# Ternary weight blocks transposed by DMA instead of TensorE, and another order in the first units of an FFN, in a fused GNN and FFN kernel

## The reference, cut to what matters

```
a = layernorm(x)
neigh = segment_sum(a[src], dst) / max(degree, 1)
h = leaky_relu(a @ W_self + neigh @ W_neigh + b)
x = x + h / max(norm(h), 1e-12)
wq = clip(round(w / scale), -1, 1) * scale      # scale: mean of |w| over 128 columns of a row, + 1e-5
y = layernorm(x)
x = x + (silu(y @ wq_gate.T) * (y @ wq_up.T)) @ wq_down.T
```

## Time and profile before

| | |
|---|---|
| median of 3 runs | 355.49 us (355.23 to 357.14) |
| the profiled execution | 353.95 us |
| its span, first to last instruction | 352.1 us |
| mean granted TensorE clock | 0.989 |
| PE busy | 330.3 us, 94% |
| DVE busy | 302.0 us, 86% |
| ACT busy | 237.6 us, 67% |
| POOL busy | 168.1 us, 48% |

### The profile page before, as it was taken

The page is one execution under the profiler, slowest core; times in us unless marked ns, Lnnn a source line. Parts: engine busy times, 40 slices in busy tenths (PEclk is TensorE's granted clock), DMA queues, the critical chain, the costliest instruction groups (busy, mean ns, idle before and its releaser), DMA issues.

```text
span 352.1 us, 5881 instructions
## 1 busy us (share of the span) xinstructions
PE 330.3 (94%) x1639; PEld 247.7 (70%) x1639; DVE 302.0 (86%) x782; ACT 237.6 (67%) x639; POOL 168.1 (48%) x234
## 2 busy tenths in 40 slices
PE   8999999999989999999569999999999999999991
PEld 3443545544444676877458898989989898899991
DVE  3799998998976269997886999999999989999993
ACT  2287887888992236765567767867668686776660
POOL 6033000000001940110023396889898888899992
PEclk9999999999999999999888999999999999999999
DMA  7982222222231011100000000000000000000205
GB/s 216 295 216 62 65 62 84 60 89 83 71 103 33 3 30 52 53 2 0 1 2 0 1 2 0 3 0 2 1 2 2 0 2 0 2 2 0 92 28 175
DMA packets 9470, 16.69 MB, mean 47 GB/s; under 512 B 1120, under 2 KB 1944, under 8 KB 9436
## 3 DMA queue, kind: packets, MB, share of 16 engines
q1 hardware_dynamic: 9358, 16.21, 15.9%
q10 hardware_dynamic: 78, 0.08, 0.1%
HBM read 13.73 MB, written 2.56 MB: 46 GB/s over the span
## 4 chain that ended last, share of the span: by engine, by line
PE 52%; DVE 13%; ACT 2%; issue 2%; POOL 1%; DVEq 0%; ACTq 0%
PE bank L1381 40%; PE bank L1312 5%; DVE tq_d L961 2%; DVE bn L1116 2%; DVE x_sb L1113 2%; PE bank L1270 1%; DVE z L1095 1%; PE bank L1294 1%; DVE z L1101 1%; PE bank L1359 1%; DVE x_lo L1131 1%; DVE acc L1169 1%; DVE g_acc L1169 1%; PE bank L1298 1%; PE bank L513 1%
## 5 line engine op out<-in xcount | busy, mean ns | idle before, releaser
L1381 PE MATMUL bank<-x_hi,t_gu 128*128 128x376 f32 (+1 forms) x264 | 95.4, 361 | 3.6 <-DVE x_lo L1131 2.8
L1381 PE MATMUL bank<-x_lo,t_gu 128*128 128x376 f32 (+1 forms) x264 | 94.3, 357 | 0.0
L1270 PE MATMUL bank<-w_sb,xnT 128*125 128x512 f32 x160 | 83.1, 607 | 0.6 <-ACT z L783 0.5
L1169 DVE SCALAR_TENSOR_TENSOR g_acc<-bank,nscale,g_acc 128x376 f32<-128x376 f32 (+1 forms) x99 | 63.9, 646 | 10.3 <-PE bank L1381 8.9
L1169 DVE SCALAR_TENSOR_TENSOR u_acc<-bank,nscale,u_acc 128x376 f32<-128x376 f32 (+1 forms) x99 | 63.7, 643 | 0.2 <-PE bank L1381 0.2
L687 POOL TENSOR_TENSOR acc<-acc,d_one 128x376 f32<-128x376 f32 (+1 forms) x58 | 63.3, 1097 | 0.0
L634 POOL TENSOR_SCALAR thr<-absum 128x4 f32<-128x4 f32 (+1 forms) x34 | 9.5, 280 | 107.3 <-ACT mag_early L744 82.9
L697 POOL TENSOR_TENSOR hh<-sg,u_acc 128x376 f32<-128x376 f32 (+1 forms) x32 | 35.1, 1096 | 53.8 <-ACT sg L889 53.2
L1381 PEld LDWEIGHTS bank<-x_hi,t_gu 128*128 128x128 f32 x264 | 50.8, 193 | 7.8 <-DVE x_lo L1131 3.5
L1381 PEld LDWEIGHTS bank<-x_lo,t_gu 128*128 128x128 f32 x264 | 50.9, 193 | 3.4
L1222 PEld LDWEIGHTS bank<-hot_dst,hot_src 128*125 128x125 bf16 x157 | 20.7, 136 | 42.3 <-DVE hot_dst L1060 28.3
(11 more groups left out here) (140 smaller groups left out, 564.5 us busy)
## 6 DMA issues: line engine op xcount, KB each, us to landing
raw<-in_L_ffn_w_gate SPq DMA_DIRECT2D x11, 256.0 KB, 2.7
raw<-in_L_ffn_w_up SPq DMA_DIRECT2D x11, 256.0 KB, 2.6
out_x<-x_sb SPq DMA_DIRECT2D x10, 224.0 KB
raw<-in_L_ffn_w_down SPq DMA_DIRECT2D x8, 256.0 KB, 2.6
w_sb<-in_L_gnn_W_neigh SPq DMA_DIRECT2D x1, 1024.0 KB, 6.1
w_sb<-in_L_gnn_W_self SPq DMA_DIRECT2D x1, 1024.0 KB, 7.3
x_sb<-in_x SPq DMA_DIRECT2D x2, 448.0 KB
raw<-in_L_ffn_w_down SPq DMA_DIRECT2D x4, 192.0 KB, 2.3
```

Source lines behind the costliest of these rows:

```text
L1169: nc.vector.scalar_tensor_tensor(out=to, in0=bank_of(u, what)[:, 0:w], scalar=nscale[:, j:j + 1], in1=to, op0=ALU.mult, op1=ALU.add).then_ ...
L1270: last = nc.tensor.matmul(to[0:TP, :], xnT[:, t, k * TP:(k + 1) * TP], w_sb[:, k, half * D:(half + 1) * D], start=k == 0, stop=k == KD - 1)
L1381: last = nc.tensor.matmul(bank_of(u, what)[:, 0:width(u)], w, parts[h], start=h == 0, stop=h == 1)
```

## The change

- Gate and up of rows 1 to 10, and down of rows 0 and 1, are no longer transposed on PE. SP issues for each block a DMA with transpose=True, 128 x 128, from tq_gu or tq_d to a new tensor turned that lies over raw, in three slots: 8 DMAs for T(f), 4 for Td(f), 88 in all. The first three events may start once raw's slot is free (a wait on ternary), each later one once the sign of the event three before has been taken (t_done). ACT waits for the DMAs' semaphore of the slot and reads turned instead of bank 7. T(0) and Td(2) to Td(10) stay on PE.
- The banks of the ring go 2, 6, 4, 5, 3, 1, 0.
- X8 is issued after U2 of unit 1 and X9 after U1 of unit 2 (both: after U3 before), T(1) has no place on PE.
- ACT: x1_high(n - 3) goes ahead of the square of turn n of the second stage; the sign of row 1 goes ahead of x1_high(7); x1_high(8) and normalize1(9) go behind the first silu; x1_high(9) behind the second.
- DVE: x1_low(n - 3) instead of x1_low(n - 4) in turn n of the second stage; shift1(9) after U1 of unit 1; x1_low(9) at the end of turn 2.

```diff
+    TURN_SLOTS = 3
+    turned = place("turned", [P, RAWS, 2 * D], BF16, "raw")
...
-        RING = [2, 6, 1, 0, 4, 3, 5]
+        RING = [2, 6, 4, 5, 3, 1, 0]
...
-        BANK7 = {(0, "U3"): ("X", 7), (1, "U1"): ("T", 1, 0), (1, "U3"): ("X", 8), (2, "U1"): ("T", 0, 1), (2, "U3"): ("X", 9),
+        BANK7 = {(0, "U2"): ("T", 1, 0), (0, "U3"): ("X", 7), (1, "U2"): ("X", 8), (1, "U3"): ("T", 0, 1), (2, "U1"): ("X", 9),
...
+        by_dma = [e for e in events if e[0] == "T" and e[1:] != (0, 0) and (not e[2] or e[1] < 2)]
+        through7 = [e for e in events if e not in by_dma]
+        def turn_slot(i):
+            return (len(loads) - RAWS + i % TURN_SLOTS) % RAWS
+        def turned_count(i):
+            return sum(16 * (KD if e[2] else 2 * KD) for e in by_dma[i % TURN_SLOTS:i + 1:TURN_SLOTS])
...
+            for i, (_, f, down) in enumerate(by_dma):
+                if i < TURN_SLOTS:
+                    sp.wait_ge(ternary, load_end[len(loads) - RAWS + i])
+                else:
+                    sp.wait_ge(t_done, turn_T[by_dma[i - TURN_SLOTS]] + 1)
+                for a in range(1 if down else 2):
+                    for k in range(KD):
+                        block = tq_d[:, k, f * P:(f + 1) * P] if down else tq_gu[:, a * NF + f, k * P:(k + 1) * P]
+                        sp.dma_start(turned[:, turn_slot(i), a * D + k * P:a * D + (k + 1) * P], block,
+                                     transpose=True).then_inc(t_turned[i % TURN_SLOTS], 16)
...
-                act.wait_ge(t_ready, turn_T["T", f, down] + 1)
+                if ("T", f, down) in by_dma:
+                    i = by_dma.index(("T", f, down))
+                    act.wait_ge(t_turned[i % TURN_SLOTS], turned_count(i))
+                    source = turned[:, turn_slot(i), 0:D if down else 2 * D]
+                else:
+                    act.wait_ge(t_ready, turn_PE["T", f, down] + 1)
+                    source = bf(7)[:, 0:D if down else 2 * D]
...
+                if n >= 3:
+                    x1_high(n - 3)
                 act.wait_ge(leaky, n + 1)
...
                 if n == 0:
                     normalize1(NT - 2)
+                    ternary_out(1, 0)
                     x1_high(7)
...
+                if n == 1:
+                    x1_high(8)
+                    normalize1(NT - 1)
+                if n == 2:
+                    x1_high(9)
...
-                if n >= 4:
-                    x1_low(n - 4)
+                if n >= 3:
+                    x1_low(n - 3)
...
-                    if n == 3 and what == "U1":
-                        x1_low(9)
+                    if n == 1 and what == "U1":
+                        shift1(NT - 1)
...
-                if n == 1:
-                    shift1(NT - 1)
-                    x1_low(8)
+                if n in (1, 2):
+                    x1_low(7 + n)
```

More of the change, by code:

```diff
@@ L119, in gnn_ffn @@
     w_sb = place("w_sb", [P, KD, 2 * D], F32, "w")
+    TURN_SLOTS = 3
+    turned = place("turned", [P, RAWS, 2 * D], BF16, "raw")
+    assert 2 * D * 2 == RW * 4
     hot_dst = place("hot_dst", [P, HOT, HOTW], BF16, "hot")
@@ L429, in gnn_ffn @@
         t_slot = [f % 2 for f in range(NF - 1)] + [2]
-        through7 = [("T", 0, 0)] + [BANK7[e] for e in sorted(BANK7)]
-        turn_T = {e: i for i, e in enumerate(e for e in through7 if e[0] == "T")}
+        events = [("T", 0, 0)] + [BANK7[e] for e in sorted(BANK7)]
+        turn_T = {e: i for i, e in enumerate(e for e in events if e[0] == "T")}
+        by_dma = [e for e in events if e[0] == "T" and e[1:] != (0, 0) and (not e[2] or e[1] < 2)]
+        through7 = [e for e in events if e not in by_dma]
+        turn_PE = {e: i for i, e in enumerate(e for e in through7 if e[0] == "T")}
+        def turn_slot(i):
+            return (len(loads) - RAWS + i % TURN_SLOTS) % RAWS
+        def turned_count(i):
+            return sum(16 * (KD if e[2] else 2 * KD) for e in by_dma[i % TURN_SLOTS:i + 1:TURN_SLOTS])
+        t_turned = [sem(f"t_turned{i}") for i in range(TURN_SLOTS)]
         piece_ready = sem("piece_ready")
@@ L830, in ternary_out @@
                 if not down:
-                    nc.scalar.activation(t_gu[:, t_slot[f], :, :].rearrange("p a d -> p (a d)"), bf(7)[:, 0:2 * D],
+                    nc.scalar.activation(t_gu[:, t_slot[f], :, :].rearrange("p a d -> p (a d)"), source,
                                          ACT.Sign).then_inc(t_done, 1)
                 else:
-                    nc.scalar.activation(t_d[:, t_slot[f], :], bf(7)[:, 0:D], ACT.Sign).then_inc(t_done, 1)
+                    nc.scalar.activation(t_d[:, t_slot[f], :], source, ACT.Sign).then_inc(t_done, 1)
             for n in range(NT):
@@ L848, in _ @@
                     root_of(n - 1)
-                if n == NT - 1:
+                if n >= 2:
                     normalize1(n - 2)
[L851 to L856, removed]
                 if n == 0:
@@ L882, in _ @@
                     root_of(NT - 1)
-                if n == 2:
-                    normalize1(NT - 1)
                 if 1 <= n <= NU:
@@ L907, in _ @@
                 if n == 1:
-                    ternary_out(1, 0)
-                    x1_high(8)
-                elif n == 2:
                     ternary_out(0, 1)
-                    x1_high(9)
                 elif n in (3, 4) and (n, "U3") in BANK7:
@@ L1148, in _ @@
             shift1(NT - 2)
-            x1_low(6)
             def take(u, what):
@@ L1382, in _ @@
                 last.then_inc(piece_ready, 1)
-                if (u, what) in BANK7:
+                if (u, what) in BANK7 and BANK7[u, what] in through7:
                     through_bank7(BANK7[u, what])
```

## The result

The changed kernel takes **344.19 us** (median of six runs, 343.11 to 344.81) against 354.71 for the kernel before, timed beside it (six runs, 353.12 to 357.14). The ratio is 0.970, 95% interval 0.966 to 0.974. The prediction was 345.2, range 342.8 to 350.0. The profiled execution of the change took 344.56, its span 342.8; before, 353.95 and 352.1.

The account below looks back on a forecast made before the run. PE was taken to bound the later rounds, with PE waiting in the first units; 0.35 + 5.6 + 0.9 + 3.4 = 10.25 us off 355.49 gave 345.2 us, range 342.8 to 350.0.

Parts of the forecast that it names:

- Part 1, T(2) to T(10): Nine groups of eight transposes leave PE's path: 3.4 us from T(4) to T(10), 0.9 from T(2) and T(3).
- rival 2: Later rounds: DVE becomes the bound; if half the gain is lost, 346.9 us; chance within the forecast's 0.66.
- Part 2, the first units: Third stage's start, up to G1 of unit 4: DVE's work sums to 22.7 us instead of 28.60; 5.6 us gained.
- Rival 1: First units don't pay: new waits at X8 and X9, slower PE clock; only 2 of 5.6 us, 348.8; chance 0.20.
- The wait at X8: First units: PE newly waits at X8 for x1_low(7) on DVE, about 2.7 us.
- X9's 1.4 us: First units: a new PE wait of about 1.4 us at X9, behind U1 of unit 2, for x1_low.
- Part 2, the second stage: x1_high ahead of the square removes tile 5's wait for xn, 0.35 us; one more x1_low before tile 9 costs nothing.
- Part 3, the DMAs: Transposing DMAs on SP cost 0, as 1.55 us a block are free and a row may take 14.0.
- the overlapping case: SP's transposing DMAs overlap as plain ones do: each costs its issue, 0.33 us, and a row 5.2 us.
- Rival 3: Blocks come too slowly by DMA: above 1.55 us each T(9) is late, at 2.6 us 421; chance 0.10.

Follow-up runs that it names:

- e1: The changed kernel with T(2) to T(10) back on PE, only T(1), Td(0) and Td(1) by DMA: 348.58 us.
- e2: The kernel before with all twelve rows by DMA, and ring, X places, ACT's and DVE's order as they were: 348.20 us.
- e6: The changed kernel with down rows 3, 5 and 7 transposed by DMA too: 343.82 us.
- e8: The changed kernel with DVE's x1_low in the second stage four tiles behind again until turn 7, (4) and (5) in turn 8: 343.49 us.
- e11: The changed kernel with down rows 3, 5 and 7 by DMA too and the second stage's x1_low four tiles behind until turn 7: 343.29 us.
- e3: The changed kernel with the ring's order of banks as before the change: 344.52 us.
- e12: The changed kernel with the old ring, old places of X8 and X9, and the second stage's x1_low(4) and (5) in turn 8, (6) in turn 9: 343.88 us.
- e5: The changed kernel with all eleven down rows transposed by DMA: 359.52 us.
- e7: The changed kernel with each 128 x 128 block as two transposing DMAs of 64 rows: 434.12 us.

## Why the prediction was right, and where it wasn't

**Part 1, T(2) to T(10): right.** Predicted 3.4 + 0.9, came 3.56 + 1.09. Each of the seven groups gave 0.51 us, its 0.46 and a little of the restart. DVE's idle time per round went from 0.72 to 0.31, not to the 0.25 I expected, and PE stayed the bound (rival 2 fell; e1 and e2 show the same from both sides).

**Part 2, the first units: right in size and in the way it was reached.** I added up DVE's work to 22.7 us; it took 22.83, with waits of 0.60 and 0.35 where 0.5 and 0.4 stood in the sum (the second is for PE here; in e6, e8 and e11 it is 0.36 for ACT's take of G0, as I had it). Rival 1, a loss of 3.6 us, didn't come. My reasons for the single parts were less good. I began with the new ring, and it is worth nothing (e3, e12); I named T(1)'s source being early, and that alone is 0.94 (e2). What let DVE run on was that ACT no longer makes PE wait behind silu and h_hi. A sum of one engine's work is right whatever removes the waits, so it couldn't tell which edit mattered. (G1 of unit 4 came at 191.60 and not near 190: the last tile's sum was 1.0 us later than before.) The wait at X8 came, 2.46 us for 2.7. **X9's 1.4 us did not come** in this profile. PE's timeline behind X8:
```profile
179.51 1.10 PE L1235 MATMUL bank<-ident,xn 125*128 125x125 f32 x4 [2.46 <-DVE x_lo L1157]
...
182.29 0.52 PE L1405 MATMUL bank<-x_hi,t_gu 128*128 128x376 f32 x1
182.60 0.41 PE L1405 MATMUL bank<-x_lo,t_gu 128*128 128x376 f32 x1
...
183.36 0.33 PE L1405 MATMUL bank<-x_lo,t_gu 128*128 128x376 f32 x1
183.53 0.59 PE L1235 MATMUL bank<-ident,xn 125*128 125x125 f32 x4
```
The matmuls up to 182.60 start 0.31 us apart, at a granted clock of 0.50 (180.0 to 182.5 us); seven of them stand there where I had four. They fill the time until x1_low(8) is done, and X9 at 183.53 doesn't wait. In e5, e6, e8 and e11 the wait at X8 is as long (2.45 to 2.46 us) and the clock stays at 1.00 behind it; there X9 waits 1.25 us, near my 1.4, and the first units take 22.8 as well. In e8:
```profile
181.37 0.65 PE L1240 MATMUL bank<-ident,xn 125*128 125x125 f32 x4 [1.25 <-DVE x_lo L1157]
```
So a part of rival 1 is true: the clock can fall behind X8. Seven slow matmuls are hidden, and eleven are in e7; in e1, where twelve stand ahead of X9 and X9 is slow too, the first units take 1.10 us more. The same wait was followed by a fall in the change, e1 and e7 and by none in four other profiles; what decides it, these runs don't show.

**Part 2, the second stage: this term failed.** I had 0.35 us of gain from tile 5's wait for xn, and wrote of the x1_low done earlier, "nothing", because DVE waits 2.17 us for PE ahead of tile 9. The stretch grew by 0.19. Tile 5's wait stayed; tile 1's shrank, and one for tile 3 came. PE's transposes that waited, before:
```profile
140.89 0.65 PE L1211 MATMUL bank<-ident,xn 125*128 125x125 f32 x4 [0.72 <-ACT xn L813]
161.95 0.62 PE L1211 MATMUL bank<-ident,xn 126*128 126x126 f32 x4 [0.42 <-ACT xn L813]
```
Now:
```profile
141.31 0.65 PE L1235 MATMUL bank<-ident,xn 125*128 125x125 f32 x4 [0.31 <-ACT xn L837]
152.18 0.62 PE L1235 MATMUL bank<-ident,xn 125*128 125x125 f32 x4 [0.51 <-ACT xn L837]
162.96 0.62 PE L1235 MATMUL bank<-ident,xn 126*128 126x126 f32 x4 [0.45 <-ACT xn L837]
```
That is 1.14 us before and 1.27 now. From about 148 to 162 us the chain of waits runs through DVE alone:
```profile
155.03 0.70 DVE bn L1142
...
156.10 0.67 DVE x_lo L1157
156.77 1.83 DVE tq_d L987 x7
158.60 0.66 DVE z L1121
```
An x1_low ahead of tq_d delays every sum behind it. And DVE's 2.2 us ahead of tile 9 are no slack for it: the chain goes on from shift on DVE (161.80) over xn and its transposes to PE's neighbour matmuls for tile 9, so PE is late there because DVE was. An x1_low is free only inside that wait; e8 puts one more there, has no wait for tile 3, and gets 0.60 us back. It then stands 0.41 under the kernel before: ACT's move is worth what I had, though not at tile 5, and the step that failed is the x1_low that I put at nothing and that cost 0.60.

**Part 3, the DMAs: the outcome right, the case wrong.** I took 0.33 us a block, "the overlapping case, as each plain issue is followed by the next long before it lands". It is 1.23 on SP, 1.29 with gaps. The cost is zero all the same, as the bound I had worked out is 1.55. The landing (2.4 us) overlaps with the next issue; it is the issue itself that is long. e5 goes past what is free: 12 blocks per row need 15.5 us where a round has 14.0, and the time rises by 15. Rival 3 was thus nearer than its 0.10: at 83% of the bound. The 1309 ns that the Trainium skill gives for a 128 x 128 transpose by DMA ("VectorE: DVE Perf Modes", The three transpose paths) agrees with the trace (1.23 us, 1.29 with gaps), and by the estimate from it, 10.5 us a row, the price would have been right (10.6 measured). Its 390 ns on TensorE isn't borne out for transposes in a stream: e1 has eight in 0.46 us, and e6 got 0.24 for each four. The 2.0 us of fixed cost in the prediction's rival 3 stand in the Trainium skill in a section on DMAs issued by GpSimd; SP's blocks here land 2.4 us after their issue and follow each other after 1.29.

**The sum.** 10.25 us predicted, 10.2 in the stretches, of which 0.8 was hidden by a later start in the profiled run. That it fits so closely is luck: the second stage fell 0.54 short of its term, and the other three came 0.17, 0.19 and 0.16 over theirs. The 345.2 is 1.0 us over the measured 344.19 mostly because I started from 355.49, the median of three runs; six runs gave 354.71.

## What to carry to other kernels

To move work to a queue that is idle, find its price per instruction on the issuing engine and hold it against the round; here the blocks of three more down rows were free and those of nine cost 15 us. Where DVE's work should bound a stretch and the stretch is longer than that work, look in the chain for a step on ACT that PE waits for, with a table load or another engine's result in front of a copy that needs neither. An idle time ahead of one instruction of a bound engine is room only for what stands right there; the same work a few instructions earlier delays the work whose lateness makes that idle time.
